# Query and key weights loaded first and in quarters, and half of ScalarE's turned time steps moved behind its copies

## The chip, the cores and the metric

The kernel runs on one core of one Trainium2 chip. The metric is the device time of one execution, in microseconds (us). Three executions of the kernel before took 424.02, 427.88 and 428.48 us; their median, 427.88 us, is the time before.

## The reference

One perceiver layer over four batches (x is 4 x 128 x 512, the context 4 x 2048 x 256), all float32:

```python
x = x + xattn(layernorm(x), ctx, ctx, Wq, bq, Wk, bk, Wv, bv)   # scores = q k^T, softmax, times v
x = x + ssm(layernorm(x), D, Lambda_re, Lambda_im, log_dt, W_re, W_im)
x = x + moe(layernorm(x), w_gate, b_gate, W1, b1, W2, b2)       # top 1 of 8 experts, relu, 512 -> 2048 -> 512
```

The second line is a convolution along each sequence with a kernel of 256 steps, `k[l, h] = Re sum_n W[h, n] exp(dt_h Lambda_n l)` with `dt = exp(log_dt)`; 128 of the steps reach the output. The kernel computes it by tables of magnitudes, `exp(-decay dt l)`, and of sines of angles. An angle is held in turns and brought to the nearest whole turn before ScalarE takes its sine.

## The kernel before

**Engines.** The program has one instruction stream for each engine, written out by hand: SyncE (SP) issues the large loads, TensorE (PE) multiplies, ScalarE (ACT) and VectorE (DVE) copy, normalize and take functions, GpSimd (POOL) takes inverse square roots. Within a stream the order is fixed, and streams meet at semaphores. `may_fill`, `did_fill`, `may_read` and `did_read` are the semaphores of the eight PSUM banks: TensorE fills, ScalarE or VectorE drains.

**Query and key weights folded.** Scores are `xn Wq Wk^T ctx^T` plus bias terms, so TensorE first makes `wqk = Wq Wk^T` (512 x 256) in four blocks d (L1287). Block d sums over four chunks e of 128 rows of `wq_sb`, against `wk_sb`, whose last column is the key bias. Each float32 product has two records in the trace, so the 16 products show as x32. Block 3 carries in addition eight one-column products with the biases (L1293) and one with `bkq_sum`, from VectorE (L1297); ScalarE copies each block out (`weights_copy`, L542 to L545).

**The query.** VectorE takes mean and variance of the four batches of x (`norm_stats`, L821 to L824), GpSimd the inverse root (L1223), VectorE the normalized rows `xn1` (L834). TensorE turns these (L1304, banks `xnT`); VectorE copies batches 0 and 2 (L850), ScalarE 1 and 3 (`turned_rows`, L549). Then TensorE makes the query's two halves (L1314), ScalarE drains the first (L560) and VectorE the second (L857), and scores of batch 0 follow (L1334). The one-column products of `key_bias` are L1321.

**Tables in the same time.** ScalarE makes the turned time steps, `turns(first, last)`: one pass of 128 x 512 each (L523), steps 1 to 15 of the coarse table before anything else, then steps 17 to 23 of the fine one. VectorE brings them to the nearest turn, two steps at a time (`a_phases(i)` and `b_phases(i)`: L795, L796), and ScalarE takes sines, four steps at a time (`a_sines(i)`, L530). `a_phases(i)` waits for steps 2i and 2i + 1; `a_sines(i)` waits for phases 2i and 2i + 1. After `a_sines(3)` ScalarE makes the magnitudes of steps 1 and 2 (`a_magnitudes`, L591) and then the softmax of batch 0 (L573), on which the turned probabilities (L1342) wait. From here on TensorE alternates turned probabilities, scores and products with the context (L1353).

**Queues.** SP issues, in this order, log_dt (for `dt_sb`), the key weights, the query weights in one load of 1 MB, x, the tables, and the context of batches 0 and 1 with the value weights between them. ACT issues five small loads before its first activation: Lambda, times, the two biases, gate weights and gate bias. The first activations wait for Lambda, times and `dt_sb` together (`params_loaded`).

Of the kernel before, what the change touches and what calls it, by code (L numbers as in the profile page):

```python
# [26 lines left out]
P = 128  # L27
NB, LQ, D = 4, 128, 512
LK, DC = 2048, 256
NS = 64  # L30
NE, DM = 8, 2048
DCH, CCH, MCH = D // P, DC // P, DM // P
# [3 lines left out]
AH, BL = 16, 8  # L36
# [30 lines left out]


K1 = 16
S_BANK = [0, 1, 2, 3]  # L70
T0, T1, T2, O_BANK = 4, 5, 6, 7

# [31 lines left out]
def perceiver_layer(nc, x, ctx, ctx_turned, wq_t, wkb_t, bkq, wv, bv, log_dt, w_ri, lam, d_skip,  # L104
# [5 lines left out]
    with ExitStack() as stack:  # L110
# [3 lines left out]
        def sem(name):  # L114
            return stack.enter_context(nc.semaphore(name))

        bank = stack.enter_context(nc.psum_tensor("bank", [P, 8, 512], F32))
# [18 lines left out]
        dt_sb = late[:, 4 * D:5 * D]  # L136
# [11 lines left out]
        ident, ones = table("ident"), table("ones")  # L148
# [22 lines left out]
        wq_sb = scratch[:, 4096:6144].rearrange("p (e d) -> p e d", e=DCH)  # L171
        u_sb = scratch[:, 4096:6144].rearrange("p (b h) -> p b h", h=D)
        q_t = scratch[:, 6144:7168].rearrange("p (c n) -> p c n", c=CCH)
        wqk = scratch[:, 7168:8192].rearrange("p (d c) -> p d c", d=DCH)
# [13 lines left out]
            return slice(HG * first, HG * last)  # L188


        wk_at = 4 * D - DCH * (DC + 1)
        wk_sb = late[:, wk_at:4 * D].rearrange("p (e c) -> p e c", e=DCH)


# [50 lines left out]
        bkq_sb = col(2 * DCH).rearrange("p (e k) -> p e k", k=2)  # L245
        bkq_prod, bkq_sum = col(DCH), col(1)
# [46 lines left out]
        place_loaded = [sem(f"place{k}_loaded") for k in range(NSLOT)]  # L293
        params_loaded, tab_loaded, x_loaded = sem("params_loaded"), sem("tab_loaded"), sem("x_loaded")
        bkq_loaded = sem("bkq_loaded")
        qk_loaded, bv_loaded, wri_loaded = sem("qk_loaded"), sem("bv_loaded"), sem("wri_loaded")
        wv_loaded, gate_loaded, d_loaded = sem("wv_loaded"), sem("gate_loaded"), sem("d_loaded")
        bias_loaded = sem("bias_loaded")
# [14 lines left out]
        xn1_ready, bkq_ready, rmax_ready = sem("xn1_ready"), sem("bkq_ready"), sem("rmax_ready")  # L313
# [37 lines left out]
        def may_fill(eng, what):  # L351

            b, n = FILL_NO[what]
            if n > 1:
                eng.wait_ge(drained[b], n - 1)
            return bank[:, b, :]

        def did_fill(ins, what):
            ins.then_inc(filled[FILL_NO[what][0]], 1)
# [60 lines left out]

        @block.sync
        def _(sp):
            sp.dma_start(dt_sb, log_dt.partition_broadcast(P)).then_inc(params_loaded, 16)
            sp.dma_start(wk_sb, wkb_t.rearrange("(e p) c -> p e c", p=P)).then_inc(qk_loaded, 16)
            sp.dma_start(wq_sb, wq_t.rearrange("(e p) d -> p e d", p=P)).then_inc(qk_loaded, 16)
            sp.dma_start(x_sb, x_rows).then_inc(x_loaded, 16)
            sp.dma_start(tab[:], tables).then_inc(tab_loaded, 16)

# [57 lines left out]
            for j in range(NSLOT, NE * UNITS):  # L486
                e, u = divmod(j - NSLOT, UNITS)
# [13 lines left out]
        def _(act):  # L501
            act.dma_start(lam_c, lam).then_inc(params_loaded, 16)
            act.dma_start(times_c, times).then_inc(params_loaded, 16)
            act.dma_start(bkq_sb, bkq.rearrange("(e p) k -> p e k", p=P)).then_inc(bkq_loaded, 16)
            act.dma_start(wg_sb[:], w_gate.rearrange("(c p) e -> p c e", p=P)).then_inc(gate_loaded, 16)
            act.dma_start(bg_sb[:], b_gate.partition_broadcast(P)).then_inc(gate_loaded, 16)
# [9 lines left out]
            def turns(first, last):  # L516

                for i in range(first, last):
                    if i < AH:
                        dst, shift = a_tab[:, :, steps_of(i, i + 1)], phase_c[:, 0:1]  # L520
                    else:
                        dst, shift = heads(b_sin1[:, i - AH, :]), phase_c[:, 1:2]
                    ins = act.activation(dst, heads(dt_sb), ACT.Identity, scale=step_ph[:, i:i + 1], bias=shift)  # L523
                    if i % 2:
                        ins.then_inc(turns_ready, 1)

            def a_sines(i):
                act.wait_ge(a_phase_ready, 2 * i + 2)
                sines = a_tab[:, :, steps_of(max(4 * i, 1), 4 * i + 4)]
                act.activation(sines, sines, ACT.Sin, scale=-TWO_PI).then_inc(a_sin_ready, 1)  # L530
# [16 lines left out]
            def turned_rows(b):  # L547
                src = may_read(act, ("xnT", b))
                did_read(act.activation(xn1_t[:, :, b * P:(b + 1) * P], src.rearrange("p (c n) -> p c n", c=DCH),  # L549
                                        ACT.Identity), ("xnT", b))  # L550

            turns(1, AH)
            for d in range(DCH):
                weights_copy(d)
            turned_rows(1)
            turned_rows(3)
            a_sines(0)
            after_read(act, ("wqk", DCH - 1))
            src = may_read(act, ("q", 0))
# [214 lines left out]
        def _(dve):  # L774
# [23 lines left out]
            def a_phases(i):  # L798
                first, last = max(2 * i, 1), 2 * i + 2
                phases(a_tab[:, :, steps_of(first, last)], by_group[:, :, steps_of(0, last - first)], i + 1, a_phase_ready)  # L800
# [35 lines left out]
                    ins.then_inc(ready, 1)  # L836

            a_phases(0)
            a_phases(1)
            dve.wait_ge(x_loaded, 16)  # L840
            which = norm_stats(range(NB))
            dve.wait_ge(bkq_loaded, 16)
            link(dve.tensor_tensor(bkq_prod, bkq_sb[:, :, 0], bkq_sb[:, :, 1], ALU.mult))
            dve.tensor_reduce(bkq_sum, bkq_prod, AX, ALU.add).then_inc(bkq_ready, 1)
            a_phases(2)
            normalized(which, range(NB), [xn1[:, b, :] for b in range(NB)], xn1_ready)

            for b in (0, 2):
                src = may_read(dve, ("xnT", b))
                did_read(dve.tensor_copy(xn1_t[:, :, b * P:(b + 1) * P], src.rearrange("p (c n) -> p c n", c=DCH)),  # L850
                         ("xnT", b))
            a_phases(3)
            a_phases(4)
            a_phases(5)
# [126 lines left out]
            for j in range(NQ):  # L981
                ins = quarter_max(0, j)
# [14 lines left out]
            ins = quarter_max(1, 3)  # L997
# [14 lines left out]
            ins = quarter_max(2, 3)  # L1012
# [15 lines left out]
            ins = quarter_max(3, 3)  # L1028
# [244 lines left out]
        def _(pe):  # L1273
            def col_slice(c):
                return slice(c * P, (c + 1) * P)
# [4 lines left out]
                for _ in range(n):  # L1280
                    pe.matmul(bank[:, O_BANK, 0:row.shape[1]], row[:, 0:P], row, start=True, stop=True)  # L1281

            pe.wait_ge(qk_loaded, 32)
            for d in range(DCH):
                dst = may_fill(pe, ("wqk", d))
                for e in range(DCH):
                    ins = pe.matmul(dst[:, 0:DC + 1], wq_sb[:, e, col_slice(d)], wk_sb[:, e, :],  # L1287
                                    start=e == 0, stop=e == DCH - 1)
                if d == DCH - 1:
                    pe.wait_ge(bkq_loaded, 16)  # L1290
                    for c in range(CCH):
                        for e in range(DCH):
                            pe.matmul(dst[:, DC + 4 + c:DC + 5 + c], wk_sb[:, e, col_slice(c)], bkq_sb[:, e, 1:2],  # L1293
                                      start=e == 0, stop=e == DCH - 1)
                    pe.wait_ge(tab_loaded, 16)
                    pe.wait_ge(bkq_ready, 1)
                    ins = pe.matmul(dst[:, DC + 6:DC + 7], ones, bkq_sum, start=True, stop=True)  # L1297
                did_fill(ins, ("wqk", d))

            for b in range(NB):  # L1300
                dst = may_fill(pe, ("xnT", b))
                pe.wait_ge(xn1_ready, b + 1)
                for c in range(DCH):
                    ins = pe.transpose(dst[:, col_slice(c)], xn1[:, b, col_slice(c)], ident)  # L1304
# [355 lines left out]
```

## Time and profile before

| what | value |
|---|---|
| runs | 424.02, 427.88, 428.48 us |
| profiled execution, its own time | 424.06 us |
| its span, first to last instruction | 422.3 us |
| PE busy | 392.0 us (93%) |
| DVE busy | 326.3 us (77%) |
| ACT busy | 262.0 us (62%) |
| mean granted TensorE clock | 0.973 |

The span is what the profile's positions are counted in; 1.8 us of the profiled execution lie outside it. That execution is near the fastest of those shown, 3.8 us below the median. Busy shares are means over the whole span and say nothing of one stage. Matmuls are pipelined: a record's own duration holds its way through the array, and how fast they follow one another is read from a row with a count.

### The profile page before, as it was taken

How to read it: one execution, taken by the hardware profiler on the slowest of the kernel's cores; microseconds unless marked ns; L12 is line 12 of the kernel's file. 1: busy time of each engine (PE TensorE's matmuls, PEld its weight loads, DVE VectorE, ACT ScalarE, POOL GpSimd, SP SyncE). 2: the span in 40 equal slices, each digit the busy share in tenths (PEclk: the TensorE clock that was granted, in tenths of full speed). 3: DMA queues.
4: the chain of work that ended last, by engine and by line, in shares of the span. 5: the costliest groups of instructions: out<-in, count | busy, mean ns of one | idle time of the engine just before them, and what ended most of it. 6: DMA issues, size and time to landing. Idle time of an engine off the chain costs nothing.

```text
span 422.3 us, 5741 instructions
## 1 busy us (share of the span) xinstructions
PE 392.0 (93%) x1650; PEld 276.9 (66%) x1650; DVE 326.3 (77%) x512; ACT 262.0 (62%) x397; POOL 58.9 (14%) x59
## 2 busy tenths in 40 slices
PE   0999999999999798869999999999999999999992
PEld 0765574757986355647777676776767777676770
DVE  2778667979464795767989899898988989898880
ACT  4859787867111012067778786877968677786850
POOL 2100000000000011040040220404003040210402
PEclk9999899999999998879999999999999999999997
DMA  8995464389426930040017999989999999950100
GB/s 221 413 417 215 192 220 178 92 339 337 135 93 261 392 144 6 2 150 25 2 22 284 371 399 400 371 303 378 343 378 372 347 385 350 370 195 1 35 5 1
DMA packets 33840, 96.56 MB, mean 229 GB/s; under 512 B 2890, under 2 KB 3530, under 8 KB 32276
## 3 DMA queue, kind: packets, MB, share of 16 engines
q1 hardware_dynamic: 30324, 90.57, 57.7%
q0 software_dynamic: 1856, 5.55, 3.8%
q10 hardware_dynamic: 1632, 0.11, 0.3%
q8 instruction: 13, 0.21, 0.2%
q14 instruction: 15, 0.12, 0.1%
HBM read 93.04 MB, written 3.68 MB: 229 GB/s over the span
## 4 chain that ended last, share of the span: by engine, by line
PE 88%; ACT 5%; DVE 2%; DMA 2%; issue 1%; POOL 1%; SPq 0%; ACTq 0%; POOLq 0%; DVEq 0%
PE bank L1531 50%; PE bank L1353 7%; PE bank L1334 5%; PE bank L1547 4%; PE bank L1363 3%; PE bank L1287 2%; DMA ring<-in_wq_t 2%; PE bank L1401 2%; PE bank L1342 2%; ACT ring L530 1%; PE bank L1408 1%; PE bank L1281 1%; ACT ring L523 1%; PE bank L1399 1%; PE bank L1501 1%
## 5 line engine op out<-in xcount | busy, mean ns | idle before, releaser
L1178 DVE TENSOR_TENSOR w_lo<-ring,w_hi 128x1024 fp32r<-128x1024 f32 x117 | 145.5, 1271 | 25.6 <-ACT w_hi L706 24.5
L706 ACT ACTIVATE w_hi<-ring 128x1024 fp32r<-128x1024 f32 x117 | 122.1, 1053 | 48.2 <-PE bank L1531 47.0
L1531 PE MATMUL bank<-w_hi,x_hi 128*128 128x512 f32 x144 | 50.4, 432 | 3.8 <-ACT w_hi L706 3.8
L1531 PE MATMUL bank<-ring,work 128*128 128x512 f32 x108 | 49.3, 592 | 0.0
L1531 PE MATMUL bank<-w_lo,x_hi 128*128 128x512 f32 x144 | 46.2, 402 | 0.0
L1531 PE MATMUL bank<-w_hi,x_lo 128*128 128x512 f32 x144 | 46.2, 402 | 0.0
L1531 PEld LDWEIGHTS bank<-w_hi,x_hi 128*128 128x128 f32 x144 | 27.1, 194 | 13.0 <-ACT w_hi L706 6.1
L1531 PE MATMUL bank<-w_hi,h_hi 128*128 128x512 f32 x90 | 33.4, 452 | 0.0
L1261 POOL TENSOR_TENSOR small<-small,x_ext 128x512 f32<-128x512 f32 x9 | 14.8, 1643 | 130.0 <-ACT small L714 130.0
L1531 PEld LDWEIGHTS bank<-w_lo,x_hi 128*128 128x128 f32 x144 | 27.6, 192 | 6.7
L1531 PEld LDWEIGHTS bank<-w_hi,x_lo 128*128 128x128 f32 x144 | 27.6, 192 | 6.7
L1531 PEld LDWEIGHTS bank<-ring,work 128*128 128x128 f32 x108 | 19.8, 190 | 18.0 <-issue 17.2
L1334 PE MATMUL bank<-ring 128*128 128x512 f32 x64 | 31.3, 621 | 0.0
L1531 PE MATMUL bank<-w_hi,h_lo 128*128 128x512 f32 x90 | 28.7, 399 | 0.0
L1353 PE MATMUL bank<-ring 128*128 128x256 f32 x128 | 28.4, 379 | 0.0
L1531 PE MATMUL bank<-w_lo,h_hi 128*128 128x512 f32 x90 | 28.2, 395 | 0.0
L1223 POOL TENSOR_TENSOR cols<-cols 128x1 f32<-128x1 f32 (+1 forms) x9 | 6.4, 715 | 153.0 <-DVE cols L824 153.0
L1353 PEld LDWEIGHTS bank<-ring 128*128 128x128 f32 x128 | 24.3, 190 | 5.0 <-issue 1.9
L1547 PE MATMUL bank<-tab,work 128*128 128x128 f32 x144 | 21.6, 272 | 0.0
L1165 DVE TENSOR_SCALAR work<-bank,small 128x128 f32<-128x128 f32 x72 | 20.3, 346 | 1.0
L1547 PEld LDWEIGHTS bank<-tab,work 128*128 128x128 f32 x144 | 17.3, 141 | 5.7 <-DVE work L1159 2.0
L1287 PE MATMUL bank<-late,ring 128*128 128x257 f32 x32 | 10.2, 492 | 11.3 <-DMA ring<-in_wq_t 11.3
(194 smaller groups left out, 616.1 us busy)
## 6 DMA issues: line engine op xcount, KB each, us to landing
ring<-in_w SPq DMA_DIRECT2D x32, 2048.0 KB, 11.0
ring<-in_ctx_turned SPq DMA_DIRECT2D x4, 2048.0 KB, 12.4
ring<-in_ctx SPq DMA_DIRECT2D x4, 2048.0 KB, 14.4
x_ext<-sorted_rows POOLq DMA_DIRECT2D x9, 257.0 KB, 3.1
work<-in_b SPq DMA_DIRECT2D x8, 256.0 KB, 7.8
ring<-in_wq_t SPq DMA_DIRECT2D x1, 1024.0 KB, 9.5
x_ext<-in_x SPq DMA_DIRECT2D x1, 1024.0 KB, 11.9
tab<-in_tables SPq DMA_DIRECT2D x1, 627.5 KB, 12.7
```

What stands on the lines that cost most here:

```text
L706: act.activation(w_hi[:, n % NSPLIT, :, :], weight_part(e, n), ACT.Identity).then_inc(hi_ready, 1)
L1165: ins = dve.tensor_scalar(hid[1][:, i * P:(i + 1) * P], bank[:, T_BANK[1], i * P:(i + 1) * P], b1_sb[:, e, m:m + 1], 0.0, ALU.add, ALU.max)
L1178: dve.tensor_tensor(w_lo[:, n % NSPLIT, :, :], weight_part(e, n), w_hi[:, n % NSPLIT, :, :], ALU.subtract).then_inc(lo_ready, 1)
L1261: pool.tensor_tensor(y_out, y_out, x_rows_w[:, 0:D], ALU.add).then_inc(y_added, 1)
L1287: ins = pe.matmul(dst[:, 0:DC + 1], wq_sb[:, e, col_slice(d)], wk_sb[:, e, :], start=e == 0, stop=e == DCH - 1)
L1334: ins = pe.matmul(dst, q_t[:, c, col_slice(b)], ctx_t[b][:, c, 512 * j:512 * (j + 1)], start=c == 0, stop=c == CCH - 1)
L1342: ins = pe.transpose(dst[:, col_slice(k)], probs[:, col_slice(KPQ * j + k)], ident)
L1353: ins = pe.matmul(dst, probs_t[:, k, :], ctx_sb[b][:, k, :], start=k == 0, stop=k == KCH - 1)
L1363: ins = pe.matmul(dst[:, i * P:(i + 1) * P], a_tab[:, 2 * wide + f % 2, :], b_tab[:, :, 2 * HG * wide:2 * HG * (wide + 1)], start=True, st ...
L1401: ins = pe.matmul(dst, an_t[:, c, :], wv_sb[:, c, :], start=False, stop=c == CCH - 1)
L1531: ins = pe.matmul(dst, kept, moved, start=start and g == 0 and q == 0, stop=stop and g == 1 and q == len(terms) - 1)
L1547: ins = pe.transpose(bank[:, T_BANK[p], col_slice(c)], hid[p][:, col_slice(c)], ident)
```

## The change

The query weights come in four loads of 128 rows, each with a semaphore of its own, and TensorE takes them chunk by chunk: the loop over e is now outside the loop over d, so that four banks are summed in turn. `log_dt` goes from SP's queue to ACT's, third after times; the biases follow it. The key weights' rows have 260 columns instead of 257 (three of them zero), and the products take 258. The biases' products come after all four blocks. On ScalarE, `turns(8, 16)` moves from ahead of the weight copies to behind the copies of the turned rows. On VectorE, `a_phases(1)` and `a_phases(2)` move behind its two copies of turned rows.

```diff
-            sp.dma_start(dt_sb, log_dt.partition_broadcast(P)).then_inc(params_loaded, 16)
             sp.dma_start(wk_sb, wkb_t.rearrange("(e p) c -> p e c", p=P)).then_inc(qk_loaded, 16)
-            sp.dma_start(wq_sb, wq_t.rearrange("(e p) d -> p e d", p=P)).then_inc(qk_loaded, 16)
+            for e in range(DCH):
+                sp.dma_start(wq_sb[:, e, :], wq_t[e * P:(e + 1) * P, :]).then_inc(wq_loaded[e], 16)
...
             act.dma_start(times_c, times).then_inc(params_loaded, 16)
+            act.dma_start(dt_sb, log_dt.partition_broadcast(P)).then_inc(params_loaded, 16)
...
-            turns(1, AH)
+            turns(1, AH // 2)
             for d in range(DCH):
                 weights_copy(d)
             turned_rows(1)
             turned_rows(3)
+            turns(AH // 2, AH)
             a_sines(0)
...
             a_phases(0)
-            a_phases(1)
             dve.wait_ge(x_loaded, 16)
             which = norm_stats(range(NB))
...
-            a_phases(2)
             normalized(which, range(NB), [xn1[:, b, :] for b in range(NB)], xn1_ready)
...
+            a_phases(1)
+            a_phases(2)
             a_phases(3)
...
-            pe.wait_ge(qk_loaded, 32)
-            for d in range(DCH):
-                dst = may_fill(pe, ("wqk", d))
+            pe.wait_ge(qk_loaded, 16)
+            for e in range(DCH):
+                pe.wait_ge(wq_loaded[e], 16)
+                for d in range(DCH):
+                    dst = may_fill(pe, ("wqk", d)) if e == 0 else bank[:, S_BANK[d], :]
+                    ins = pe.matmul(dst[:, 0:DC + 2], wq_sb[:, e, col_slice(d)], wk_sb[:, e, 0:DC + 2],
+                                    start=e == 0, stop=e == DCH - 1)
+                    if e == DCH - 1 and d < DCH - 1:
+                        did_fill(ins, ("wqk", d))
+            pe.wait_ge(bkq_loaded, 16)
+            for c in range(CCH):
                 for e in range(DCH):
-                    ins = pe.matmul(dst[:, 0:DC + 1], wq_sb[:, e, col_slice(d)], wk_sb[:, e, :],
-                                    start=e == 0, stop=e == DCH - 1)
...
+                    pe.matmul(dst[:, DC + 4 + c:DC + 5 + c], wk_sb[:, e, col_slice(c)], bkq_sb[:, e, 1:2],
+                              start=e == 0, stop=e == DCH - 1)
+            pe.wait_ge(tab_loaded, 16)
+            pe.wait_ge(bkq_ready, 1)
+            did_fill(pe.matmul(dst[:, DC + 6:DC + 7], ones, bkq_sum, start=True, stop=True), ("wqk", DCH - 1))
```

## Rows read from the trace of the kernel before

**Rows 1.** Chain that ended last, whole span (the page's part 4).
```profile
PE 88%; ACT 5%; DVE 2%; DMA 2%; issue 1%; POOL 1%; SPq 0%; ACTq 0%; POOLq 0%; DVEq 0%
```
**Rows 2.** The chain's pieces from 0 to 80 us: start, length, what.
```profile
1.79 9.52 DMA ring<-in_wq_t
...
11.35 10.15 PE bank L1287 x32
21.50 1.68 PE bank L1293 x16
23.18 0.22 PE bank L1297 x2
23.41 1.82 PE bank L1304 x16
...
25.25 0.61 ACT ring L549
...
26.09 3.69 PE bank L1314 x8
...
44.25 0.78 PE bank L1342 x4
```
**Rows 3.** The chain inside 12.78 to 17.06 us, then inside 17.43 to 21.12 us.
```profile
12.57 4.71 PE bank L1287 x11
...
17.28 4.00 PE bank L1287 x18
```
**Rows 4.** DMA issues: KB each, us from issue to landing.
```profile
ring<-in_wq_t SPq DMA_DIRECT2D x1, 1024.0 KB, 9.5
tab<-in_tables SPq DMA_DIRECT2D x1, 627.5 KB, 12.7
late<-in_wkb_t SPq DMA_DIRECT2D x1, 514.0 KB, 5.9
```
**Rows 5.** Timeline of SP's issues: start, length, engine, line.
```profile
1.32 0.42 SPq L424 DMA_DIRECT2D late<-in_wkb_t  x1
...
3.18 0.92 SPq L427 DMA_DIRECT2D tab<-in_tables  x1
```
**Rows 6.** Timeline of ScalarE; in brackets its idle time before.
```profile
7.71 10.69 ACT L523 ACTIVATE ring<-late,cols 128x512 f32<-128x512 f32 x15 [0.52 <-DVE cols L787]
...
29.86 0.69 ACT L560 ACTIVATE ring<-bank,cols 128x512 f32<-128x512 f32 x1 [1.22 <-PE bank L1314]
```
**Rows 7.** Timeline of VectorE.
```profile
14.28 0.69 DVE L821 BATCH_NORM_STATS2 cols<-x_ext 128x6 f32<-128x512 f32 x1 [2.36 <-DMA x_ext<-in_x]
...
18.06 0.17 DVE L824 TENSOR_SCALAR cols<-cols 128x4 f32<-128x4 f32 x1
...
19.14 1.23 DVE L796 TENSOR_TENSOR ring<-small,ring 128x1024 f32<-128x1024 f32 x1
20.28 1.91 DVE L834 TENSOR_SCALAR ring<-x_ext,cols 128x512 f32<-128x512 f32 x4
...
25.42 0.68 DVE L795 TENSOR_SCALAR small<-ring 128x1024 f32<-128x1024 f32 x1
...
33.31 0.75 DVE L857 TENSOR_SCALAR ring<-bank,cols 128x512 f32<-128x512 f32 x1 [1.83 <-PE bank L1314]
```
**Rows 8.** Timeline of GpSimd: the first inverse root and the second.
```profile
18.41 1.60 POOL L1223 TENSOR_TENSOR cols<-cols 128x4 f32<-128x4 f32 x1 [14.29 <-DVE cols L824]
...
71.12 0.55 POOL L1223 TENSOR_TENSOR cols<-cols 128x1 f32<-128x1 f32 x1 [51.11 <-DVE cols L824]
```
**Rows 9.** ScalarE alone by stretch: length, busy (instructions), clock, DMA share, GB/s.
```profile
29.90:43.50 13.60, 13.57 (x15) 1.00 0.63 243
```
**Rows 10.** By stretch: length; PE, PEld, DVE, ACT, POOL busy (instructions); granted clock; DMA share; GB/s.
```profile
40.80:44.25 3.45, 2.73 (x26) 2.65 (x24) 2.12 (x7) 3.42 (x7) 0.00 (x0) 1.00 0.60 176
...
44.64:48.05 3.41, 3.41 (x7) 1.40 (x6) 1.01 (x1) 2.10 (x6) 0.00 (x0) 0.50 0.93 389
```

More of the change, by code:

```diff
@@ L69 @@
 K1 = 16
+WK = DC + 4
 S_BANK = [0, 1, 2, 3]
@@ L188, in steps_of @@
             return slice(HG * first, HG * last)
-        wk_at = 4 * D - DCH * (DC + 1)
+        wk_at = 4 * D - DCH * WK
         wk_sb = late[:, wk_at:4 * D].rearrange("p (e c) -> p e c", e=DCH)
@@ L295, in perceiver_layer @@
         bkq_loaded = sem("bkq_loaded")
+        wq_loaded = [sem(f"wq{e}_loaded") for e in range(DCH)]
         qk_loaded, bv_loaded, wri_loaded = sem("qk_loaded"), sem("bv_loaded"), sem("wri_loaded")
@@ L1281, in keep_warm @@
                     pe.matmul(bank[:, O_BANK, 0:row.shape[1]], row[:, 0:P], row, start=True, stop=True)
-            pe.wait_ge(qk_loaded, 32)
-            for d in range(DCH):
-                dst = may_fill(pe, ("wqk", d))
-                for e in range(DCH):
-                    ins = pe.matmul(dst[:, 0:DC + 1], wq_sb[:, e, col_slice(d)], wk_sb[:, e, :],
-                                    start=e == 0, stop=e == DCH - 1)
[L1289 to L1298, printed above, removed]
+            pe.wait_ge(qk_loaded, 16)
[9 more added lines that the diff above has]
+            for c in range(CCH):
+                for e in range(DCH):
+                    pe.matmul(dst[:, DC + 4 + c:DC + 5 + c], wk_sb[:, e, col_slice(c)], bkq_sb[:, e, 1:2],
[3 more added lines that the diff above has]
+            did_fill(pe.matmul(dst[:, DC + 6:DC + 7], ones, bkq_sum, start=True, stop=True), ("wqk", DCH - 1))
             for b in range(NB):
@@ L1635 @@
         "wq_t": g["L0_xattn_Wq"].T,
-        "wkb_t": np.concatenate([g["L0_xattn_Wk"].T, g["L0_xattn_bk"][:, None]], 1),
+        "wkb_t": np.concatenate([g["L0_xattn_Wk"].T, g["L0_xattn_bk"][:, None], np.zeros((D, WK - DC - 1), np.float32)], 1),
         "bkq": np.stack([g["L0_xattn_bk"], g["L0_xattn_bq"]], 1),
```

## The prediction

> **What bounds the kernel now.** The chain of waits comes first: 88% of the span lies on TensorE and 5% on ScalarE [rows 1]. So almost everything is a row of matmuls, and a change can only pay where the chain is on something else, or where matmuls run slowly. The chain's first 45 us show where that is [rows 2]. It starts on the load of the query weights, which land at 1.79 + 9.52 = 11.3 us; then come the weight products (11.35 to 21.5), their small biases (1.68 + 0.22), the turned rows of x (1.82), ScalarE's last copy of them (25.25, 0.61, so until 25.86) and the first half of the query (26.09 to 29.78). The first turned probabilities stand in the chain at 44.25. What lies between is not TensorE: in the stretch from 29.90 to 43.50 ScalarE is busy for 13.57 of 13.60 us [rows 9]. So there are two stages with different limits. Until 29.8 us it is the load, the products and the copies; from 29.8 to 44.25 us it is ScalarE's list of turned steps, sines and magnitudes. After that TensorE goes on without a wait for long, so I carry a shift of 44.25 to the end one to one.
>
> Two rows on matmul rates complete this. Inside the weight products, the first 11 records shown take 4.71 us (0.428 each), the last 18 take 4.00 us (0.222 each, 0.217 without the first) [rows 3]. One is twice the other: the first is TensorE at the lower of its two levels (1.2 GHz), the second at the higher (2.4 GHz). The rate changed at about 17.1 us, 5.7 us after the first matmul.
>
> **The loads.** The key weights are issued at 1.32 and land 5.9 us later, at 7.2; the query weights land at 11.3 [rows 4, 5]. Taking log_dt off SP's queue does not take it off the 16 DMA engines: it now runs on ACT's queue beside the key weights. Its 256 KB still have to be moved ahead of the last quarter. I therefore leave the key weights at 7.2 and the last quarter at 11.3, and space the quarters evenly: (11.3 - 7.2)/4 = 1.0 us, so 8.2, 9.3, 10.3 and 11.3. Bounds for the first quarter: 7.0 if log_dt gives way, 10 if it is slow and shared. The padding of 6 KB costs nothing beside 1.5 MB. `params_loaded` may come later than now (the turned steps start at 7.71 [rows 6]), but only seven of them stand before the weight copies, 7 x 10.69/15 = 5.0 us, so up to 3 us of delay are hidden by the wait for the weights. Three more issues on SP at 0.4 us each push x's issue to about 3.1 us, far ahead of its turn on the engines; x should land at 14.26 as now, since the same bytes are ahead of it.
>
> **The weight products.** They start at 8.2 us instead of 11.35. A quarter is 8 records, 3.4 us at the lower rate, longer than the 1.0 us between quarters, so TensorE doesn't starve. With the same 5.7 us before the rate rises (13.9 us), 13 records are done by then and 19 are left: 19 x 0.217 = 4.1 us, so 18.0 us. That is 3.5 us earlier than 21.5. 258 columns instead of 257 are 0.4% of this, nothing. The biases add 1.68 + 0.22, giving 19.9; the sum on VectorE that they need comes at about 18.5 us as before, and the tables land at 3.18 + 12.7 = 15.9 [rows 4, 5].
>
> **The normalized rows.** They are the second input of the turned rows, and have been hidden so far. Statistics run from 14.28 to 18.2, then GpSimd's root took 1.60 us (18.41 to 20.0), and the four rows another 1.91 us, to 22.2 [rows 7, 8]. If this stayed, turned rows could not be complete before 21.95 + 0.44. But later roots took 0.55 us [rows 8]; during the first one VectorE ran two passes of 1024 elements on SBUF, L795 and L796 [rows 7], and exactly those move away. I take 0.55, with 1.60 as the other end: rows normalized at 19.0 + 1.9 = 20.9, so TensorE is the later one, and its 16 transposes end at 19.9 + 1.9 = 21.8. By the Trainium skill (GPSIMD Engine Reference, Key points) GpSimd shares its SBUF interfaces with VectorE and is slowed by instructions in a 2-port mode or with two SBUF inputs, which speaks for the short root. Were the 1.60 a cost of the first call instead, the sum would be 0.65 us higher.
>
> ScalarE's last copy then ends at about 22.5 instead of 25.86, and the query starts 3.3 us earlier. This is the whole gain of the change.
>
> **What it costs: the moved turned steps.** Eight passes of 0.713 us, 5.7 us [rows 6], left a place where they were hidden behind the load and the products. They now lie between 22.5 and 28.2 us. `a_sines(0)` follows as before: 29.86 - 1.22 - 25.86 = 2.8 us [rows 2, 6], until 31.0. The query's first half is complete at about 26.3 and waits for ScalarE; its copy ends at 31.65 instead of 30.55. So ScalarE enters its full stretch 1.1 us later: 5.70 added, 3.36 regained, 1.22 regained from the wait ahead of L560. In that stretch nothing is idle [rows 9] and nothing is removed, so the turned probabilities start 1.1 us later, at 45.35. Queued behind the late copy on ScalarE are all sines and magnitudes; who waits for it is TensorE's scores of batch 0, which end at about 39.5 all the same (the second half is drained at about 33.3, see below), so they don't bind.
>
> **VectorE** now has five phase pairs between its copies (to 22.4) and the query's second half, where it had three. A pair is 2.0 us (L857 is preceded by 25.42 + three pairs = 31.5 and 1.83 us of idle time [rows 7]), so it drains that half at 22.4 + 5 x 2.03 + 0.75 = 33.3, against 34.06. Its phases stay ahead of ScalarE's sines by over 3 us. No cost.
>
> **The clock behind it.** Between 40.80 and 44.25 TensorE had one-column products only, and then ran from 44.64 to 48.05 at half of its clock, 1.2 GHz [rows 10]; that cost 1.7 us of that stretch. Now the one-column products begin 1.3 us earlier and the probabilities 1.1 us later, so the light stretch grows from 3.4 to 5.9 us. The nearest row for a return from no load at all is the start: 5.7 us at the lower rate [rows 3], a loss of 2.9 us, 1.2 more than 1.7. A reason for a gain is absent, since a longer light stretch can't raise the clock. I take the 1.2, the ends are 0 and 1.4.
>
> **Sum** for an execution like the profiled one: 424.06 + 1.1 + 1.2 = 426.4 us, with the ends 424.7 (products first at 7.0, where the rows of x hold the copy at 22.0; clock 0) and 428.4 (products first at 10, so 1.8 more; clock 1.4). The profiled execution lies 3.8 us under the median of those shown; of four times two are near 424 and two near 428, so their mean is 426.1, and I put the forecast at 426.1 + 2.3 = 428.4 us.
>
> **Rivals.**
> - *The gain is kept* (faster). ScalarE's moved steps would have to be covered, and the light stretch to keep the clock up: 426.1 - 3.3 - 1.7 = 421.1. Against it stands the row with 13.57 of 13.60 us busy; for it only that the front is plainly shorter. Chance 0.12.
> - *Even* (no change). The last turned row is copied by 21.4 us instead of 22.5, from which point the steps moved cost nothing. It needs the first quarter at 7.0 and x half a microsecond earlier. Time 426.1. Chance 0.15.
> - *Starved products* (slower). The quarters come late or uneven, because log_dt's 128 copies of one row share the engines with them, and TensorE stays at 1.2 GHz for all 32 records: first matmul 9.5, end 9.5 + 32 x 0.428 = 23.2, copy of the last row at 27.7, probabilities at 45.35 + 5.2 = 50.5. Time 426.1 + 6.3 + 1.2 = 433.6. It decides once the products end after 21.5. The evenly falling landings speak against it. Chance 0.12.
> - *A fixed price for each load.* With 2.6 us between quarters the last lands at 7.2 + 10.4 = 17.6; 8 x 0.217 follow, so the products end at 19.4 instead of 18.0, and the total is 429.8. The tables, 627 KB, landed only 1.6 us after x, so a price of that size is not paid in line. It is the Trainium skill (DMA: Bandwidth & Descriptors, Anatomy of one DMA) that gives about 2.0 us fixed for each DMA plus its bytes, 2.6 us for a quarter by its fit; the trace shows it overlapped. Chance 0.05.
> - *The forecast:* 0.56.
>
> **How the numbers follow.** A change under 1% (4.3 us) is about what runs of this kernel can't tell from none. Within it lie the forecast, the even case and the load case, 0.76, less a little for the spread of single executions (4.5 us); faster takes the first rival and some spread, 0.13; slower takes the starved products and some spread, 0.15; the same keeps 0.72. The range goes from 423.5 (even case, fast execution) to 433 (the highest run shown, 428.5, plus the sum's upper end of 4.3).
>
> **What would show it.** In the trace after: first L1287 near 8.2 us and last near 18; the first L1223 near 0.55 us; ScalarE's L523 in a group of eight from about 22.5, without idle time from there to the first L573; copy L560 ending near 31.6; the first L1342 near 45.3, and a granted clock of 0.50 behind it. The prediction is wrong if ScalarE has idle time between L549 and L573, if L1342 starts before 44.2, or if x lands a microsecond earlier.

## The result and the profile after

The changed kernel took 430.92 us (median of 6 runs, 429.66 to 431.49) where the kernel before took 426.51 us (6 runs, 422.34 to 428.48). The two medians are 4.4 us apart, 1.0%; the ratio on record, an estimate of its own and not their quotient, is 1.0158, 95% interval 1.0119 to 1.0196. A second measurement, with 12 runs of the changed kernel and 35 of the kernel before, gave 1.007 (1.003 to 1.011), medians 427.66 and 424.30 us. All of these say slower, by 0.7% to 1.6%; how far the runs explain the difference is told below. The ratios leave out executions more than 1.5% above the fastest of their kernel (at most five of twelve, and one of 1026.42 us in "turns back"), while the medians keep them.

The profiled execution took 429.66 us with a span of 428.0 us. First the page's clock row and its chain by engine:

```profile
PEclk9989699999999998799999999999999999999997
...
PE 83%; ACT 7%; DVE 3%; DMA 3%; issue 2%; POOL 1%; SPq 1%; ACTq 0%; POOLq 0%; DVEq 0%
```

TensorE's share of the chain fell from 88% [rows 1] to 83%, and what came in is ScalarE, VectorE, loads and waits without a name. Each digit of the clock row stands for a fortieth of the span, 10.7 us. It has a dip in its fifth digit (43 to 53 us), where the kernel before had one too, and a small one in its third (21 to 32 us).

The chain's pieces of the first 80 us (start, length, what) show the stages, to be held against [rows 2]:

```profile
3.42 10.83 DMA x_ext<-in_x
...
14.28 0.70 DVE cols L826
...
18.41 1.05 POOL cols L1228
...
20.09 3.42 PE bank L1310 x16
...
23.53 0.60 ACT ring L553
24.12 3.97 ACT ring L527 x6
...
32.55 0.58 ACT ring L565
...
46.10 0.67 ACT ring L578 x2
...
46.82 1.11 PE bank L1348 x4
```

The load of the query weights and the weight products have left the chain. It now begins with x, goes through the statistics on VectorE, GpSimd's root and the transposes (the turned rows of x, L1310), and from 23.53 us on it is ScalarE up to the first turned probabilities. These start at 46.82 us, 2.6 us later than the 44.25 of before, although ScalarE's last copy of turned rows ends 1.7 us earlier (24.13 against 25.86).

TensorE by time (start, length, and in brackets the idle time before):

```profile
5.88 3.78 PE L1293 MATMUL bank<-late,ring 128*128 128x258 f32 x8 [5.88 <-DMA ring<-in_wq_t]
10.37 5.49 PE L1293 MATMUL bank<-late,ring 128*128 128x258 f32 x24 [0.72 <-DMA ring<-in_wq_t]
15.70 1.84 PE L1300 MATMUL bank<-cols,late 128*128 128x1 f32 x16
18.62 0.35 PE L1304 MATMUL bank<-cols,tab 128*128 128x1 f32 x2 [1.08 <-DVE cols L848]
20.09 3.40 PE L1310 MATMUL bank<-tab,ring 128*128 128x128 f32 x16 [1.11 <-DVE ring L839]
```

The products end at 15.9 us, 5.6 us earlier than before. Then TensorE has one-column products, two waits of 1.1 us, and the transposes, which take 3.4 us where they took 1.8 [rows 2]. The reason is in the clock; here are three stretches (length; PE, PEld, DVE, ACT, POOL busy; granted clock; DMA share; GB/s):

```profile
17.00:20.42 3.42, 1.23 (x10) 1.09 (x11) 2.27 (x9) 0.51 (x3) 1.05 (x1) 1.00 1.05 439
20.42:23.83 3.41, 3.07 (x15) 2.66 (x13) 2.73 (x6) 0.90 (x2) 0.00 (x0) 0.50 1.00 428
44.31:51.14 6.83, 4.32 (x8) 2.15 (x9) 0.83 (x1) 4.99 (x11) 0.00 (x0) 0.50 0.43 184
```

In the first stretch TensorE was busy for 1.23 of 3.42 us; then it had 1.2 GHz instead of 2.4 for the transposes. The last row is the second dip, 6.8 us long where it was 3.4 [rows 10].

The loads (KB each, us from issue to landing) answer to [rows 4]:

```profile
ring<-in_wq_t SPq DMA_DIRECT2D x4, 256.0 KB, 8.3
x_ext<-in_x SPq DMA_DIRECT2D x1, 1024.0 KB, 10.8
...
late<-in_wkb_t SPq DMA_DIRECT2D x1, 520.0 KB, 4.0
...
late<-in_log_dt ACTq DMA_DIRECT2D x1, 256.0 KB, 7.6
```

The key weights are there at 4.9 us instead of 7.2, log_dt only at 9.4, and x at 14.25, unchanged.

From 51 us to 159 us the matmuls lie 3.0 us later than before. The span differs by 5.7. Nearly all of the other 2.7 us comes in one piece, ahead of the second window of experts, in the chain (start, length, what):

```profile
235.79 6.05 PE bank L1537 x19
...
241.92 1.06 ACT w_hi L711
242.99 1.13 issue
244.12 5.85 PE bank L1537 x24
```

At the same place the chain of before has TensorE without a break. "Issue" is time in which TensorE waited for nothing that the profile shows; the timeline puts its whole idle time there at 2.3 us.

### The profile page after: what moved, and what is told of

Read it like the earlier page. It is cut to its first block, busy times and chain, and to the rows that moved or that the text cites. A ratio compares the mean times of both kernels' runs of the same rounds, so it can differ in the third digit from the quotient of the medians.

```text
span 428.0 us, 5745 instructions
## 1 busy us (share of the span) xinstructions
PE 393.6 (92%) x1650; PEld 277.9 (65%) x1650; DVE 325.4 (76%) x512; ACT 261.7 (61%) x397; POOL 56.7 (13%) x59
## 4 chain that ended last, share of the span: by engine, by line
PE 83%; ACT 7%; DVE 3%; DMA 3%; issue 2%; POOL 1%; SPq 1%; ACTq 0%; POOLq 0%; DVEq 0%
PE bank L1537 50%; PE bank L1359 6%; PE bank L1340 5%; PE bank L1553 4%; PE bank L1369 3%; DMA x_ext<-in_x 3%; ACT ring L527 2%; PE bank L1407 2%; PE bank L1348 2%; ACT ring L534 1%; PE bank L1414 1%; PE bank L1286 1%; PE bank L1405 1%; PE bank L1383 1%; PE bank L1438 1%
## 5 line engine op out<-in xcount | busy, mean ns | idle before, releaser
L711 ACT ACTIVATE w_hi<-ring 128x1024 fp32r<-128x1024 f32 x117 | 122.0, 1053 | 49.7 <-PE bank L1537 48.7
L1537 PE MATMUL bank<-w_hi,x_lo 128*128 128x512 f32 x144 | 45.7, 399 | 0.0
L1537 PE MATMUL bank<-w_hi,h_hi 128*128 128x512 f32 x90 | 33.3, 452 | 0.0
L729 ACT ACTIVATE work<-bank,small 128x128 f32<-128x128 f32 x72 | 20.2, 362 | 0.0
## 6 DMA issues: line engine op xcount, KB each, us to landing
ring<-in_ctx_turned SPq DMA_DIRECT2D x4, 2048.0 KB, 12.1
```

The source lines that it names most:

```text
L711: act.activation(w_hi[:, n % NSPLIT, :, :], weight_part(e, n), ACT.Identity).then_inc(hi_ready, 1)
L729: ins = act.activation(hid[0][:, i * P:(i + 1) * P], bank[:, T_BANK[0], i * P:(i + 1) * P], ACT.Relu, bias=b1_sb[:, e, m:m + 1])
L1537: ins = pe.matmul(dst, kept, moved, start=start and g == 0 and q == 0, stop=stop and g == 1 and q == len(terms) - 1)
```

## The experiments

The landmarks of each profile are: the end of ScalarE's last copy of turned rows, the end of its copy of the query's first half, the start of the first softmax, the start of the first turned probabilities, and the start of the first gate matmul. "Stall" is TensorE's idle time ahead of the second window of experts.

| kernel | last copy | query copy | softmax | probabilities | gate | stall | profiled us | median us (runs) | ratio to before |
|---|---|---|---|---|---|---|---|---|---|
| before | 25.8 | 30.6 | 43.4 | 44.3 | 155.9 | none | 424.06 | 426.51 (6) | 1 |
| before, again | 24.6 | 29.3 | 42.2 | 43.0 | 155.8 | none | 424.60 | 425.60 (10) | 1.0003 (0.996 to 1.004) |
| changed | 24.1 | 33.1 | 46.0 | 46.8 | 158.9 | 2.3 | 429.66 | 430.92 (6) | 1.0158 (1.012 to 1.020) |
| changed, again | 24.5 | 33.5 | 46.4 | 47.2 | 159.9 | 2.1 | 431.11 | 427.66 (12) | 1.007 (1.003 to 1.011) |
| turns back | 24.1 | 28.8 | 42.5 | 43.3 | 155.0 | none | 423.17 | 427.92 (12) | 1.0044 (1.000 to 1.009) |
| turns only | 26.0 | 35.0 | 47.9 | 48.7 | 160.1 | none | 427.58 | 429.13 (6) | 1.0127 (1.007 to 1.018) |
| four moved | 23.2 | 30.0 | 42.9 | 43.7 | 155.4 | 2.5 | 428.43 | 426.20 (12) | 0.999 (0.995 to 1.003) |
| log_dt on SP | 23.8 | 32.8 | 45.7 | 46.5 | 159.0 | none | 427.81 | 430.75 (11) | 1.0119 (1.008 to 1.016) |
| long fillers | 24.6 | 33.6 | 46.4 | 52.4 | 162.3 | none | 431.07 | 431.31 (6) | 1.0154 (1.011 to 1.020) |
| short fillers | 23.2 | 32.3 | 45.1 | 46.3 | 156.3 | none | 422.40 | 422.58 (12) | 0.9968 (0.994 to 1.000) |
| before, filled | 25.2 | 29.9 | 42.8 | 43.6 | 153.6 | 2.8 | 426.92 | 426.65 (12) | 1.0012 (0.997 to 1.005) |
| no moves | 23.8 | 28.5 | 41.4 | 42.2 | 152.1 | 3.3 | 425.37 | 425.17 (12) | 1.0013 (0.998 to 1.004) |
| back, filled | 24.6 | 29.3 | 44.4 | 46.4 | 156.3 | none | 425.09 | 424.87 (12) | 0.998 (0.994 to 1.002) |
| no moves, filled | 24.0 | 28.8 | 41.6 | 42.5 | 152.4 | none | 421.24 | 423.77 (12) | 0.9957 (0.991 to 1.000) |

A single execution strays by some microseconds (the kernel before: 422.2 to 429.8), so what a part is worth is read from the landmarks; the ratios say whether it shows in the time. The ratios come from four measurements, each with its own executions of the kernel before.

Two differences of landmarks help to read the table. From the probabilities to the gate it is 109.9 to 110.0 us in six profiles, where the clock stays up behind the probabilities, and 111.4 to 112.7 us in the other eight, where it is at one half for a while: a dip there costs 1.4 to 2.8 us. From the gate to the end of the span it is 264.5 to 267.2 us in the nine profiles without a stall and 269.1 to 271.6 us in the five with one.

**Turns back.** The moved steps returned, all else as changed:

```diff
-            turns(1, AH // 2)
+            turns(1, AH)
...
-            turns(AH // 2, AH)
             a_sines(0)
```

> The changed kernel with ScalarE's turned steps 8 to 15 back ahead of its weight copies; loads, products and VectorE as changed. Theory (the moved steps cost what they displace): ScalarE makes 15 steps from 10.7 to 21.4 us, its last copy of turned rows ends near 24.1 as in the changed kernel, the query's first half is drained near 28.7 instead of 33.0, and the first L1348 starts near 43.1 (set by VectorE's maxima, 42.4) instead of 46.8; 3.7 us and up to 1.7 us of slow clock less, so 425 to 427 us where the changed kernel has 430.9. Rival (the loads and their effect on the clock are what costs): within 1.5 us of the changed kernel, 429.5 or more.

The last copy ends at the same 24.1 us, the query's copy 4.4 us earlier (28.8), the probabilities 3.5 us earlier (43.3, expected 43.1), the gate 3.9 us earlier. That is as the theory had it, in the trace. The time is neither the theory's 425 to 427 us nor the rival's 429.5: 427.92 us, which is 3.0 under the changed kernel's first median and about equal to its second. What it doesn't do is beat the kernel before, although its gate lies 0.9 us earlier.

**Turns only.** The kernel before with this move alone (the reverse of the diff above).

> The kernel before with nothing but the move of ScalarE's turned steps 8 to 15 behind the turned rows. Theory (the moved steps cost what they displace): the copy of turned rows ends near 25.9 as before, 5.7 us of steps follow, of which 1.2 us take the place of a wait: the query's first half is drained near 35.0 instead of 30.5, the first L1342 starts near 48.7 instead of 44.25, and the slow clock after it lasts longer: plus 4.5 to 6.5 us on the kernel before. Rival (loads are what costs): plus 0 to 1 us.

ScalarE's timeline (start, length, operation):

```profile
25.39 0.60 ACT L549 ACTIVATE ring<-bank 128x512 f32<-128x512 f32 x1 [0.28 <-PE bank L1305]
25.89 5.74 ACT L523 ACTIVATE ring<-late,cols 128x512 f32<-128x512 f32 x8
31.64 1.28 ACT L530 ACT_TABLE_LOAD   x1
32.94 1.48 ACT L530 ACTIVATE ring<-ring 128x1536 f32<-128x1536 f32 x1
34.33 0.67 ACT L561 ACTIVATE ring<-bank,cols 128x512 f32<-128x512 f32 x1
```

The eight passes fill 5.74 us without a break, and the query's copy ends at 35.0, as expected to a tenth. The probabilities start at 48.7 (expected 48.7), and the ratio is plus 1.27%, 5.4 us. At the landmarks this single edit costs more than the whole change (probabilities at 48.7 against 46.8, gate at 160.1 against 158.9), so the rest of the change gains, and the move is what loses.

**Four moved.** Steps 12 to 15 alone behind the turned rows: `turns(1, 12)` in front, `turns(12, AH)` behind.

```diff
-            turns(1, AH // 2)
+            turns(1, 12)
...
-            turns(AH // 2, AH)
+            turns(12, AH)
```

> The changed kernel with only turned steps 12 to 15 behind the turned rows, 8 to 11 back in front. Theory (each moved step costs its 0.71 us on ScalarE's full stretch): the last copy of turned rows still ends near 24.1, the first half of the query is drained near 30.3 (28.8 with none moved, 33.1 with eight; four of them less fill a wait), the first L1348 starts near 44.0: about 2.9 us less than the changed kernel, 424 to 425 us. Rival (a fixed price for the second group of steps, however many): near 46.8 as in the changed kernel.

The query's copy ends at 30.0 (expected 30.3) and the probabilities start at 43.7 (44.0), against 28.8 and 43.3 with none moved and 33.1 and 46.8 with eight: no fixed price for the second group of steps. How the price divides is less plain, for the last copy of turned rows ended at 23.2 here and not at 24.1 as expected. Counted from that copy, the query's copy ends 4.7 us later with none moved, 6.8 with four and 9.0 with eight. With four, TensorE made the query at half clock (9.2 us for 16 records instead of 7.1), so that ScalarE still waited 0.55 us for it. The time can't be told from the kernel before: ratio 0.999.

**log_dt on SP.** The load at the head of SP's queue again, all else as changed.

```diff
+            sp.dma_start(dt_sb, log_dt.partition_broadcast(P)).then_inc(params_loaded, 16)
             sp.dma_start(wk_sb, wkb_t.rearrange("(e p) c -> p e c", p=P)).then_inc(qk_loaded, 16)
...
-            act.dma_start(dt_sb, log_dt.partition_broadcast(P)).then_inc(params_loaded, 16)
```

> The changed kernel with log_dt back at the head of SP's queue, all else as changed. Theory 1 (the products, begun early, end early and leave TensorE without work from 15.7 to 20.1 us, so its clock falls and the 16 transposes take 3.4 us instead of 1.8): here the key weights land near 7.3, the first quarter near 8.3, the products end near 18, TensorE has no gap of more than 1 us before the transposes, they take 1.8 us, ScalarE's last copy ends near 22.3 instead of 24.1 and the first L1348 starts near 45.1 instead of 46.8: 1.6 us less than the changed kernel. Theory 2 (log_dt beside the weights costs nothing): no difference within 0.5 us and the clock falls here too.

Neither theory holds as a whole. The products ran from 10.3 us (expected 8.3), for the quarters landed at 10.2, 10.7, 11.3 and 12.1 us; they ended at 19.4, and the transposes took 1.9 us at the full clock. Theory 1's link holds: without the empty stretch ahead of them there is no dip at 20 us. But the gain is 0.4 us at the last copy and not 1.8, since the transposes start 1.1 us later. A dip came at 34.6 us instead, inside the scores. The queue that log_dt is in is worth little either way.

**Long and short fillers.** Here matmuls whose results nobody uses are put where TensorE has nothing to do (`keep_warm`). First with 512 columns, two, three and eight:

```diff
+            keep_warm(2, wq_sb[:, 0, :])
             pe.wait_ge(bkq_loaded, 16)
...
             did_fill(pe.matmul(dst[:, DC + 6:DC + 7], ones, bkq_sum, start=True, stop=True), ("wqk", DCH - 1))
+            keep_warm(3, tab[:, 0:4 * P])
...
             key_bias(1, range(1, NB))
+            after_read(pe, ("qb", 0))
+            keep_warm(8, tab[:, 0:4 * P])
```

> The changed kernel with matmuls added whose results are not used: two (512 columns) after the weight products, three after the product with bkq_sum, and eight after key_bias of batches 1 to 3, where TensorE has nothing else. Theory (1.6 us of the loss are the transposes at half clock and 1.9 us are the matmuls after the first softmax at half clock): transposes take 1.8 us, the last copy of turned rows ends 1.6 us earlier, the first L1348 starts near 45.2, and the four L1340 records behind it take 1.7 us instead of 3.4: 3.0 to 3.5 us less than the changed kernel, about as fast as the kernel before. Rival (the clock is a by-product and ScalarE alone sets the pace): no more than 1 us less.

A miss of its design: one such product is two records of 0.43 us, twice what I had counted, so the eight took 8.8 us and the probabilities started at 52.4. The transposes did take 1.9 us, but began only at 22.0, behind the fillers. The clock was at one half from 44.8 to 48.3 us in spite of the eight. Then with 256 columns, two, three, two ahead of `key_bias` and three behind it:

```diff
+            keep_warm(2, wq_sb[:, 0, 0:2 * P])
             pe.wait_ge(bkq_loaded, 16)
...
+            keep_warm(3, tab[:, 0:2 * P])
...
+            after_read(pe, ("qb", 0))
+            keep_warm(2, tab[:, 0:2 * P])
             key_bias(1, range(1, NB))
+            keep_warm(3, tab[:, 0:2 * P])
```

> The changed kernel with shorter fillers of 256 columns whose results are not used: two matmuls after the weight products, three after the product with bkq_sum, two ahead of key_bias of batches 1 to 3 and three behind it (each 0.43 us at the full clock). Theory (half clock costs 1.6 us in the transposes and 1.9 us behind the first L1348): transposes 1.9 us instead of 3.4, last copy of turned rows near 22.6, first L1348 near 45.3, four L1340 records behind it 1.7 us: 3 us less than the changed kernel. Rival (ScalarE's list alone): less than 1 us.

Two stretches of it, the transposes and the four records behind the first turned probabilities, here with those behind the second (columns as above):

```profile
20.70:22.60 1.90, 1.90 (x17) 1.67 (x15) 1.72 (x4) 0.60 (x1) 0.00 (x0) 1.00 1.01 431
46.26:50.66 4.40, 4.40 (x18) 2.38 (x16) 1.96 (x3) 3.45 (x9) 0.00 (x0) 0.98 0.13 54
```

The first is at full clock, the second nearly. But the second dip wasn't prevented: the clock was at one half from 43.0 to 46.3 us, ahead of the probabilities, and it fell on the fillers. Four of their records ahead of `key_bias`, and six behind it, took (start, length):

```profile
39.84 1.03 PE L1286 MATMUL bank<-tab 128*128 128x256 f32 x4
...
43.56 2.91 PE L1286 MATMUL bank<-tab 128*128 128x256 f32 x6
```

The last copy ends 0.9 us earlier than in the changed kernel and the gate 2.6 us earlier; the probabilities only 0.6 (46.3, expected 45.3), since those slowed fillers ran into them. The ratio is 0.9968 where the changed kernel had 1.007 in the same measurement, 4.3 us for matmuls that compute nothing. Not all of it is the front: eleven of the twelve executions lie between 421.9 and 424.9 us, so the upper group of times that the changed kernel has (see below) is all but missing. Against its lower group the gain is 3.2 us. The theory's 3 us were reached in the time, and the rival's 1 us exceeded.

For the transposes the fillers' effect stands on seven profiles. Where the products end early and nothing fills the gap, the transposes take 2.8 to 3.7 us (changed twice, turns back, four moved); with fillers in the gap 1.9 us (long, short, back filled).

**Before, filled.** Two such products ahead of `key_bias`, in the kernel before.

```diff
+            after_read(pe, ("qb", 0))
+            keep_warm(2, tab[:, 0:2 * P])
             key_bias(1, range(1, NB))
```

> The kernel before with two 256-column matmuls whose results are not used between the scores of batch 0 and key_bias of batches 1 to 3. The stretch of one-column products is then 2.7 us long with work on both sides. Theory (that stretch is what lowers the clock): no 0.50 row behind the first L1342, 1.7 us less than the kernel before, at most 0.2 us spent. Rival (the clock falls with any such stretch): L1342 0.2 us later and the clock falls as before, so no gain.

In the trace there is no dip behind the probabilities, and the gate is at 153.6 instead of 155.9 and 155.8: 2.2 to 2.3 us. In the time there is nothing, neither the theory's 1.7 us nor a loss: 1.0012, and that without the five slowest of twelve. Its executions lie at 421.1 to 429.2, and its profile has the stall. So a front gain of 2 us can vanish in what follows.

**No moves.** Quarters, loop order and late biases, with log_dt on SP and every turned step and `a_phases(1)` in front. Against the changed kernel, beside the two edits of log_dt above:

```diff
-            turns(1, AH // 2)
+            turns(1, AH)
...
-            turns(AH // 2, AH)
...
             a_phases(0)
+            a_phases(1)
             dve.wait_ge(x_loaded, 16)
...
-            a_phases(1)
             a_phases(2)
```

> The changed kernel's quarters, loop order and late biases alone: log_dt at the head of SP's queue, all 15 turned steps ahead of the weight copies, a_phases(1) ahead of the statistics; only a_phases(2) stays behind the turned rows. Theory (the loads and products are worth 2 us and the moved steps cost 5.7 less a wait): the last copy of turned rows ends near 23.8 instead of 25.8, the query's first half is drained near 28.5, the first L1348 starts near 42.3 instead of 44.25: about 2 us less than the kernel before. Rival (the front is worth nothing because VectorE's maxima come no earlier): L1348 near 44 and no difference.

The probabilities start at 42.2 (expected 42.3), the last copy ends at 23.8 and the query's copy at 28.5: the loads and late biases are worth 2.1 us at the query's copy against the first profile of before and 0.9 against the second. The gate lies 3.6 to 3.8 us earlier than in both. 1.7 to 2.8 us of that is the clock, which stays up behind the probabilities here although nothing fills the gap: 24 one-column products, 0.72 us of idle time, and no dip. The time is 1.0013: again nothing, with a stall of 3.3 us in the profile.

**Back, filled.** The edit of "turns back", with the short fillers but for the last three.

> The changed kernel with two things at once: the turned steps 8 to 15 back ahead of the weight copies, and fillers of 256 columns whose results are not used (two after the weight products, three after the product with bkq_sum, two ahead of key_bias of batches 1 to 3). Theory (the two costs found are separate and add up): transposes at full clock, ScalarE's first half of the query drained near 28, the first L1348 near 43 (set by VectorE's maxima), full clock behind it: 3 us less than the kernel with fillers alone, so near 420 us and faster than the kernel before by 1%. Rival (what the front gains is lost to VectorE's five phase pairs): no faster than 422.6.

The costs didn't add up, and the rival's bound (no faster than 422.6 us) was kept: 424.87 us. The clock fell at 35.2 us, inside the scores, after a stretch in which TensorE waited for the query's second half:

```profile
31.80 0.95 PE L1328 MATMUL bank<-cols,ring 128*128 128x1 f32 x8
32.61 1.10 PE L1341 MATMUL bank<-ring 128*128 128x512 f32 x2
35.08 7.97 PE L1341 MATMUL bank<-ring 128*128 128x512 f32 x14 [1.37 <-DVE ring L861]
```

Fourteen records took 8.0 us where they take 6.3 in "turns back". VectorE, with its five phase pairs, drains that half from 34.3 to 35.0 us, and TensorE waits 1.4 us for it (0.9 us in "turns back"): this is the place where those pairs cost something. The ratio, 0.998, doesn't tell it from the kernel before.

**No moves, filled.** The edit of "no moves", with the one of "before, filled".

> Quarters, loop order and late biases with log_dt on SP, all turned steps in front and a_phases(2) alone moved, and two 256-column matmuls with unused results ahead of key_bias of batches 1 to 3. Theory: the first L1348 near 42.3 as without the fillers and no slow clock behind it in any execution: 421 to 424 us, 1 to 3 us less than the kernel before. Rival (executions differ by the stall before the second window of experts, and not by the clock at 45 us): as without the fillers, 425.

The probabilities start at 42.5, the gate at 152.4, and there is no dip before 160 us, as in "no moves" itself; so these two fillers aren't shown to do anything for the clock here. The two profiles have the same front within 0.3 us, one with a stall of 3.3 us and one without, and their spans are 423.7 and 419.5 us: that is the plainest price of the stall, 4.2 us. The median is 423.77 us, the ratio 0.9957 (0.9914 to 1.0000), and the profile the fastest of all, 421.24 us. This version and the short fillers have the lowest ratios, with intervals that end at 1.0000 and 0.9999, barely clear of the kernel before if at all.

**Changed, again, and before, again.** Both without an edit.

> The changed kernel once more, unchanged. Its first profile had TensorE idle for 2.3 us at 241.8 us, ahead of the second window of experts, with 1.1 us in which nothing shown is waited for. If that stands in every execution of this program, it is 2.6 us of the change's price, and the second profile shows it at the same matmul. If it is an accident of one execution, it is absent here, and the first L1348 at 46.8 (plus 2.6 us) and the slow clock behind it (plus 0.4) are what lasts: a profiled time near 427.

> The kernel before once more, unchanged, for its second profile. Theory (TensorE's stall ahead of the second window of experts is an accident that the kernel before has too, in about a third of its executions, and it is what parts its times near 424 from those near 428): the profiled time is near 424 without a gap over 1 us there, or near 428 with one of 2 to 3.5 us. Rival (the stall belongs to the changed program): never here.

The changed kernel has its stall again (2.1 us, up to 245.6), now with the probabilities at 47.2 and the clock at one half from 18.7 to 28.9 us. The kernel before has none in either profile. But the stall isn't the changed program's own: its relatives have it or not (table), and it stands in a kernel that adds nothing but fillers to the kernel before.

The traces hold one more sign of it. They list packets of the kind "instruction", on a queue q8 among others. All nine profiles without a stall have one such packet between 202 and 213 us. The five with a stall have none between 190 and 235 us; theirs comes at 235.2 to 242.5 us, within 1 us of the start of TensorE's idle time, takes 1.0 us, and another follows 5.6 to 5.9 us behind. In TensorE's program the windows of the experts are a loop with a branch ahead (`pe.If`, `pe.Fori`). So the stall goes with instructions that are loaded late. That TensorE waits for them is my reading; which engine these packets serve, and why they are sometimes late, no trace shows.

The times show two groups: of 35 executions of the kernel before in that measurement 23 lie at 422.5 to 425.4 (median 423.7) and 12 at 427.0 to 429.8 (428.3); of the changed kernel's 12, six at 424.8 to 427.0 (425.8) and six at 428.3 to 431.6 (430.4). Where the changed kernel's groups part is a choice (427.0 and 428.3 us are neighbours). Group against group the change costs 2.1 us.

## Why the prediction was wrong

It forecast 428.4 us, 2.3 above the 426.1 it took for the kernel before, and no change beyond 1%. Measured were 430.92 us, 4.4 above the kernel before's median, and a ratio of plus 1.6% (0.7% in the second measurement). The main mechanism was right, that the moved steps cost more than the earlier products give; its sum was too small, because one term had the wrong clock, and the stall wasn't in it.

- **The moved steps: right.** 5.7 us in front of the sines, one wait filled; turns only and turns back show it from both sides (plus 4.4 and minus 4.4 us at the query's copy), with four moved in between. The even case and the kept gain are ruled out.
- **"so TensorE is the later one, and its 16 transposes end at 19.9 + 1.9 = 21.8": the step that failed.** Measured: 20.09 + 3.40 = 23.5, so ScalarE's last copy ended at 24.1 instead of 22.5 and the probabilities started at 46.8 instead of 45.35. TensorE wasn't the later one: it waited 1.1 us for the normalized rows, which come out of x, the statistics and the root. That moved the start by only 0.2 us; the other 1.5 us is the length. I had priced the transposes at the clock of before and asked for the clock only where I already knew a dip. The early end of the products made a new stretch with little work, 1.23 us busy in 3.42, and the dip fell on the transposes. Fillers in that stretch bring them back to 1.9 us in three profiles of three.
- **The root: too short.** It took 1.05 us instead of 0.55 in all ten profiles where VectorE's two large passes had moved away, against 1.60 in the four where they ran beside it. The passes explain half of the difference to 0.55. The Trainium skill (GPSIMD Engine Reference, Key points) names a sharing of SBUF interfaces with VectorE; the traces agree in direction, by 0.55 us. The first root is also the only one with four columns and the first of its kind; which of these costs the other 0.5 us, no run tells.
- **The loads: wrong, without effect.** log_dt on ACT's queue did give way: the key weights came at 4.9 and the first quarter at 5.8, my lower bound being 7.0, but the others at 10.3 to 11.4, which made one wait of 0.72 us; the products ended at 15.9 instead of 18.0. The last three landed 0.3 and 0.8 us apart, so a fixed price of 2.6 us that is paid one load after the other is ruled out. `params_loaded` came 3 us late, just within what I had called hidden: the seven steps end at 15.76 us, as the copies can begin. With the 15 steps in front (turns back) they run until 21.8 instead of 18.4, and ScalarE's copies follow without a break to 24.1. Even so this delay costs little, for the transposes, at half clock, end at 23.3 there and would have held the last copy until 23.9.
- **VectorE: right** for the changed kernel (second half drained at 34.1, forecast 33.3, with ScalarE setting the pace), although "turns back" and "back, filled" show how near it is: there TensorE waits 0.9 and 1.4 us for it.
- **The clock behind the probabilities: within its bounds, but the reason isn't shown.** Plus 1.2 was forecast within 0 to 1.4; from the probabilities to the gate the two profiles take 0.4 and 1.1 us more than the first of before. I had put it down to the longer stretch of light work, yet the second profile of before, whose stretch didn't grow, also takes 1.1 us more. The kernel before has no fixed value there.
- **What wasn't in the sum.** By the trace the front costs 3.0 us (gate 158.9 against 155.9; in the second profile 4.0), 0.7 more than forecast. The other 2.7 us of the profiled execution is nearly all the stall. For the 4.4 us between the first measurement's medians that is likely too, but not shown, since only profiled executions have a trace: all six runs of the changed kernel lay in its upper group, and three of six of the kernel before in theirs. I had seen two levels near 424 and 428 and treated them as scatter that is shared alike; with six runs each they needn't be. Whether the changed kernel is in its upper group more often (12 of 18 executions in these two measurements, against 15 of 41) because of the change or by chance stays open.

## What to carry to other kernels

When work is moved out of a place where it was hidden, price it where it lands: here eight passes landed in a run of one engine without idle time, and every one of them counted. When a stage is made to start early but the next input doesn't come earlier, ask what TensorE does in the gap, and don't take the clock of the stage after it from the old trace; here the gap cost the transposes 1.5 us, and five useless matmuls in it brought 0.9 us back at the last copy. And where the times of a kernel fall in two groups, compare group with group before a difference of 1% is explained.

## What the runs showed of the hardware

- A 256 KB load that copies one row to 128 partitions took 3.5 us at the head of SP's queue and 7.6 us on ACT's queue beside SP's 1.5 MB; the key weights landed 1.9 us sooner after their issue for it (4.0 against 5.9 us).
- Of four quarters issued within 2.0 us the first landed at 5.8 us and the last three at 10.3 to 11.4. With log_dt ahead of them on their own queue they landed at 10.2, 10.7, 11.3 and 12.1.
- TensorE's clock fell to one half after stretches with one-column products and short waits, at 20.4, 35.2 and 44.3 us in various kernels, at places that moved from execution to execution. Its longest idle time ahead of the first of these was 1.1 us. It doesn't always fall: in "no moves" the same 24 one-column products and 0.72 us of idle time were followed by the full clock.
- Fillers don't hold the clock for certain either: with five products of 256 columns around the one-column products it was at one half from 43.0 to 46.3 us.
- TensorE stalled for 2.1 to 3.3 us ahead of the second window of experts in five of fourteen profiles. In the other nine an instruction packet of queue q8 ran at 202 to 213 us; in these five it came only as the stall began.
